# RNN input products of eight steps by seven block products, in a fused RNN and LSTM kernel on one Trainium2 core

## The reference

```python
# layer 0 (RNN), h0 = cond_1024
xW = einsum('ntd,dh->nth', x, WxR) + bR
h_t = tanh(h_{t-1} @ WhR + xW_t)
y = x + h
# layer 1 (LSTM), starts at zero
a = y_t @ WxL + bL + h_{t-1} @ WhL           # 2048 columns: i, f, o, g
c = sigmoid(f) * c + sigmoid(i) * tanh(g)
h = sigmoid(o) * tanh(c)
out = y + h
```

## Time and profile before

| | |
|---|---|
| median of 3 runs | 846.36 us (844.5 to 847.37) |
| profiled execution | 844.77 us, span of its core 843.0 us |
| TensorE busy | 827.6 us (98%), 22859 matmuls |
| TensorE's stationary loads | 620.9 us (74%) |
| VectorE / ScalarE / GpSimd busy | 602.5 / 578.9 / 289.0 us |
| granted TensorE clock | full (2.4 GHz) over the whole span |

### The profile page before, as it was taken

The page is one execution under the profiler, slowest core; times in us unless marked ns, Lnnn a source line. Parts: engine busy times, 40 slices in busy tenths (PEclk is TensorE's granted clock), DMA queues, the critical chain, the costliest instruction groups (busy, mean ns, idle before and its releaser), DMA issues.

```text
span 843.0 us, 52000 instructions
## 1 busy us (share of the span) xinstructions
PE 827.6 (98%) x22859; PEld 620.9 (74%) x22859; DVE 602.5 (71%) x1722; ACT 578.9 (69%) x1542; POOL 289.0 (34%) x642
## 2 busy tenths in 40 slices
PE   8899999999999999999999999999999999999997
PEld 5555555677787777877778777787777877778896
DVE  3668778877777776777677777668776776767664
ACT  5986476767676667767767776677767767677652
POOL 1312366723323323333332332333333233333320
PEclk9999999999999999999999999999999999999999
DMA  8801100111001111001111000111110000000001
GB/s 309 281 18 27 29 15 16 28 28 26 19 18 30 29 30 29 16 16 30 29 29 29 23 24 17 29 29 30 29 26 20 17 16 17 16 16 16 11 11 28
DMA packets 40195, 30.70 MB, mean 36 GB/s; under 512 B 5772, under 2 KB 38688, under 8 KB 38688
## 3 DMA queue, kind: packets, MB, share of 16 engines
q1 hardware_dynamic: 39712, 27.27, 11.3%
q10 hardware_dynamic: 256, 0.11, 0.0%
HBM read 18.95 MB, written 8.39 MB: 32 GB/s over the span
## 4 chain that ended last, share of the span: by engine, by line
PE 90%; DMA 4%; DVE 3%; ACT 2%; issue 1%; SPq 0%; ACTq 0%; DVEq 0%
PE ps_l L1290 34%; PE ps_l L1356 29%; PE ps_r L1442 9%; PE ps_r L1462 8%; PE ps_l L1334 3%; PE ps_l L1303 2%; PE ps_l L1323 2%; DMA wxl_raw<-in_L_cond_Wx 2%; DMA whl_raw<-in_L_cond_Wh 2%; DMA whr_raw<-in_L_cond_Wh 1%; PE ps_r L1413 1%; PE ps_r L1424 1%; DVE ig L1092 0%; PE ps_l L1277 0%; DVE fc L1090 0%
## 5 line engine op out<-in xcount | busy, mean ns | idle before, releaser
L496 POOL TENSOR_TENSOR xb<-xb,h_l 128x128 f32<-128x128 f32 x127 | 58.2, 458 | 383.8 <-DVE h_lo L1125 379.4
L1090 DVE TENSOR_TENSOR fc<-gates,c 128x128 f32<-128x128 f32 x128 | 39.6, 309 | 150.4 <-ACT gates L780 136.5
L1356 PE MATMUL ps_l<-whl_raw,wxl_raw 128*32 128x256 f16 x3816 | 131.6, 273 | 0.0
L1290 PE MATMUL ps_l<-whl_hi,hT_hi 128*32 128x512 f16 x1888 | 122.5, 379 | 1.1 <-DVE hT_hi L1109 1.1
L1290 PE MATMUL ps_l<-whl_hi,hT_lo 128*32 128x512 f16 x1888 | 122.5, 379 | 0.0
L1290 PE MATMUL ps_l<-whl_lo,hT_hi 128*32 128x512 f16 x1888 | 122.4, 379 | 0.0
L1356 PE MATMUL ps_l<-wxl_hi,wxl_raw 128*32 128x256 f16 x2544 | 115.8, 273 | 0.0
L1356 PEld LDWEIGHTS ps_l<-whl_raw,wxl_raw 128*32 128x32 f16 x3816 | 102.1, 97 | 2.2 <-issue 0.2
L780 ACT ACTIVATE gates<-ps_l,g_products 128x256 f32<-128x256 f32 x114 | 53.5, 469 | 54.2 <-PE ps_l L1290 54.1
L1290 PEld LDWEIGHTS ps_l<-whl_lo,hT_hi 128*32 128x32 f16 x1888 | 51.1, 97 | 50.8
L1290 PEld LDWEIGHTS ps_l<-whl_hi,hT_lo 128*32 128x32 f16 x1888 | 51.1, 97 | 50.8
(11 more groups left out here) (215 smaller groups left out, 1820.6 us busy)
## 6 DMA issues: line engine op xcount, KB each, us to landing
xb<-in_x SPq DMA_DIRECT2D x128, 64.0 KB, 2.2
out<-xb SPq DMA_DIRECT2D x124, 64.0 KB, 1.8
whl_raw<-in_L_cond_Wh SPq DMA_DIRECT2D x4, 1024.0 KB, 6.6
wxl_raw<-in_L_cond_Wx SPq DMA_DIRECT2D x4, 1024.0 KB, 6.0
wxr_raw<-in_L_cond_Wx SPq DMA_DIRECT2D x1, 1024.0 KB, 5.4
whr_raw<-in_L_cond_Wh SPq DMA_DIRECT2D x1, 1024.0 KB, 7.4
out<-xb SPq DMA_DIRECT2D x4, 48.0 KB, 2.2
wxl_raw<-peaks SPq DMA_DIRECT2D x5, 2.0 KB, 2.6
```

Source lines behind the costliest of these rows:

```text
L496: nc.gpsimd.tensor_tensor(xb[g % NX][:, t, :], xb[g % NX][:, t, :], h_l[s % 2][:, :], ALU.add).then_inc(out_done, 1)
L1290: last = nc.tensor.matmul(ps_l[s % 4][quarter(j), :], (hT_hi, hT_lo)[h_part][:, k, :], gate_slice(whl[w_part][k], j), start=False, stop=(h ...
L1356: last = nc.tensor.matmul(at[quarter(j), :], stationary, weights[:, j, :, :], start=False, stop=(y_part == 1 and k == 1), skip_group_check ...
```

## The change

From RNN step 48 on (XQ = 6, blocks q = 6 to 15 of eight steps) the input products are made for eight steps at once. The two groups of four steps are the two rows of a 2 x 2 block matrix, the two halves of the contraction its columns; WxR is cut into 2 x 2 blocks too. Instead of eight block products (8 * 24 matmuls) seven are made (7 * 24), one in each of the ticks 8q - 9 to 8q - 3, in the place of `product_r16`; in tick 8q - 2 there is none. They are accumulated in two PSUM banks (`ps_pk`, `ps_end`). Around them are added, for each q:

- GpSimd: four sums of 128x256 (`x_sum`, ticks 8q - 11 and 8q - 9).
- ScalarE, behind `rnn_h_hi` at the end of a tick: in 8q - 10 two high halves of 128x512 and a seed, in 8q - 9 a copy, a seed and a high half of 128x256, in 8q - 8 a copy and a high half of 128x512, in 8q - 7 a copy, in 8q - 4 and 8q - 3 a whole bank of 128x512 out of PSUM (`take_x`).
- VectorE, behind everything else of a tick: the two turns of x in 8q - 14 and 8q - 12 (before: ahead of the RNN's turn, in ticks 4g - 4), the low halves in 8q - 10 and 8q - 8, two additions in PSUM in 8q - 6 and 8q - 4.
- SyncE: twice eight transfers inside SBUF that bring the results to the partitions where the RNN's recurrent product wants them (`x_inputs`), beside zeros. `seed_xin` puts them into the RNN's PSUM bank in the place of the bias.

`x16_hi`, `x16_lo` and `product_r16` end before step 48. The blocks of WxR are made once, in ticks 27 to 33. The batches of x scales now hold two groups each from group 12 on, and come eight ticks earlier. From tick 27 on the RNN state's low half is made ahead of the LSTM's cell (fc, ig, c), not behind it. Two scale constants go from 2^-14 to 2^-12.

```diff
+XQ = 6
+GX = 2 * XQ
-        BATCHES = [(G1, 3)] + [(g, 4) for g in range(4, NG, 4)]
+        BATCHES = [(G1, 3), (4, 4), (8, 4)] + [(g, 2) for g in range(GX, NG, 2)]
-        TURN_X_AT.update({4 * g - 4: g for g in range(3, NG)})
+        TURN_X_AT.update({4 * g - 4: g for g in range(3, GX)})
-        X16_AT.update({4 * g - 2: g for g in range(RG + 1, NG)})
+        X16_AT.update({4 * g - 2: g for g in range(RG + 1, GX)})
+        LOW_FIRST = 27
+        X_ORDER = (1, 5, 6, 2, 7, 3, 4)
+        def ahead(k, ticks):
+            q = (k + ticks) // 8
+            return q if (k + ticks) % 8 == 0 and XQ <= q < NG // 2 else None
...
+            def x_inputs(q, half):                                   # SyncE
+                sp.wait_ge(x_out, 2 * (q - XQ) + half + 1)
...
+                for t in range(TG):
+                    for c in (0, 1):
+                        sp.dma_start(xin[quarter(c), 4 * half + t, :, :], ...)
...
+                if ahead(k, 11) is not None:                         # GpSimd
+                    x_sum(ahead(k, 11), 1)
+                    x_sum(ahead(k, 11), 2)
+                if ahead(k, 9) is not None:
+                    x_sum(ahead(k, 9), 3)
+                    x_sum(ahead(k, 9), 4)
...
-                if RS <= k + 2 < T:                                  # ScalarE
+                if RS <= k + 2 < 8 * XQ:
                     seed_r(k + 2)
+                if 8 * XQ <= k + 2 < T:
+                    seed_xin(k + 2)
                 if R0 - 1 <= k < T - 1:
                     rnn_h_hi(k)
+                for i in XW_HALVES_AT.get(k, []):
+                    wxr_high(i)
+                if ahead(k, 10) is not None:
+                    x_top_high(ahead(k, 10))
+                    x_sums_high(ahead(k, 10), 0)
+                    seed_xa(ahead(k, 10))
+                if ahead(k, 9) is not None:
+                    copy_xm1(ahead(k, 9))
+                    seed_xd(ahead(k, 9))
+                    x_22_high(ahead(k, 9))
+                if ahead(k, 8) is not None:
+                    take_xm5(ahead(k, 8))
+                    x_sums_high(ahead(k, 8), 1)
+                if ahead(k, 7) is not None:
+                    copy_xu2(ahead(k, 7))
+                if ahead(k, 4) is not None:
+                    take_x(ahead(k, 4), 0)
+                if ahead(k, 3) is not None:
+                    take_x(ahead(k, 3), 1)
...
+                    if LOW_FIRST <= k < T:                           # VectorE
+                        rnn_h_lo(k - 1)
                     cell(k - LAG)
...
-                    if R0 <= k < T:
+                    if R0 <= k < LOW_FIRST:
                         rnn_h_lo(k - 1)
                     hidden(k - LAG)
...
+                if ahead(k, 14) is not None:
+                    turn_block(2 * ahead(k, 14))
+                if ahead(k, 12) is not None:
+                    turn_block(2 * ahead(k, 12) + 1)
...
+                if ahead(k, 10) is not None:
+                    x_top_low(ahead(k, 10))
+                    x_sums_low(ahead(k, 10), 0)
+                if ahead(k, 8) is not None:
+                    x_22_low(ahead(k, 8))
+                    x_sums_low(ahead(k, 8), 1)
...
-                elif r < T:                                          # TensorE, next_product_r
+                elif r < 8 * XQ:
                     product_r16(r)
+                for i, n in enumerate(X_ORDER):
+                    if ahead(r - 1, 9 - i) is not None:
+                        x_block(ahead(r - 1, 9 - i), n)
```

More of the change, by code:

```diff
@@ L163, in rnn_lstm_kernel @@
         ps_end = bank("ps_end")
+        ps_x = [ps_pk, ps_end]
         s_h0 = sem("h0_loaded")
@@ new lines, in x_top_high @@
+            def x_top_high(q):
+                act.wait_ge(xg_turned, 2 * (q - XQ) + 2)
+                group_scales(act, 2 * q)
+                if q == XQ:
+                    input_product_done(act, S2 - 1)
+                    act.wait_ge(y_split, G2 - G1)
+                else:
+                    x_products_done(act, q - 1, 2)
+                nc.scalar.activation(xs_top[0], x_row(2 * q), ACT.Copy,
+                                     scale=g_scale_r[:, OF_X, 2 * q:2 * q + 1]).then_inc(xs_high, 1)
@@ L757, in rnn_h_hi, with take_x @@
+            def take_x(q, half):
+                x_products_done(act, q, 4 if half else 3)
+                wait(act, xin_loaded[half], DMA * 2 * TG * (q - XQ))
+                nc.scalar.activation(x_wide[half], ps_x[half][:, :], ACT.Copy).then_inc(x_out, 1)
             def rnn_h_hi(r):
@@ L1209, in _ @@
                     add_u3(pair_at(k - 1))
+                if ahead(k, 14) is not None:
+                    turn_block(2 * ahead(k, 14))
+                if ahead(k, 12) is not None:
+                    turn_block(2 * ahead(k, 12) + 1)
+                for i in XW_HALVES_AT.get(k, []):
+                    wxr_low(i)
+                if ahead(k, 10) is not None:
[4 more added lines that the diff above has]
+                    x_sums_low(ahead(k, 8), 1)
+                if ahead(k, 6) is not None:
+                    add_xm5(ahead(k, 6))
+                if ahead(k, 4) is not None:
+                    add_xu3(ahead(k, 4))
                 if k == T:
@@ L1430, in quadrant_of_r16, with x_block @@
                 return w[:, chunk * H:(chunk + 1) * H].rearrange("p (m c u) -> p c m u", m=2, c=2)[:, c, :, :]
+            def x_block(q, n):
+                done = 4 * (q - XQ)
+                if n == 1:
+                    pe.wait_ge(xs_split, done + 1)
+                    pe.wait_ge(xa_seeded, q - XQ + 1)
+                elif n == 5:
+                    if q == XQ:
+                        pe.wait_ge(xw_split, J)
+                    pe.wait_ge(xs_split, done + 2)
+                    pe.wait_ge(xd_seeded, q - XQ + 1)
+                elif n == 6:
+                    pe.wait_ge(xm1_copied, q - XQ + 1)
+                elif n in (2, 7):
+                    pe.wait_ge(xs_split, done + 4)
+                    pe.wait_ge(xm5_out, q - XQ + 1)
+                    pe.wait_ge(xu2_copied, q - XQ + 1)
+                elif n == 3:
+                    pe.wait_ge(xb_sum, q - XQ + 1)
+                else:
+                    pe.wait_ge(xd_sum, q - XQ + 1)
+                out = {1: (0, 0), 2: (0, 0), 6: (0, 1), 3: (0, 1), 5: (1, 1), 7: (1, 0), 4: (1, 0)}[n]
+                cols = slice(out[1] * HALF, (out[1] + 1) * HALF)
+                x_home, x_at = {1: (xs_top, 0), 2: (xs_top, HALF), 4: (xs_22, 0), 5: (xs_sums, 0), 6: (xs_sums, HALF),
+                                7: (xs_sums, 2 * HALF), 3: (xs_sums, 3 * HALF)}[n]
+                w_home, w_row, w_at = {1: (wr[OF_X], 0, 0), 2: (wr[OF_X], 2, HALF), 3: (wr[OF_X], 2, 0), 5: (tx, 0, 0),
+                                       7: (tx, 0, HALF), 6: (tx, 2, 0), 4: (tx, 2, HALF)}[n]
+                for x_part, w_part in ((0, 0), (0, 1), (1, 0)):
+                    for k in (0, 1):
+                        first = (w_row + k) * H + w_at
+                        for t in range(TG):
+                            at = x_at + k * P + t * B
+                            last = nc.tensor.matmul(ps_x[out[0]][quarter(t), cols], x_home[x_part][:, at:at + B],
+                                                    w_home[w_part][:, first:first + HALF], start=False,
+                                                    stop=(x_part == 1 and k == 1), skip_group_check=True)
+                last.then_inc(xp_mm, 1)
             def recurrent_r16(r):
```

214 lines of the change are left out of this document (202 added, 12 removed).

## The result

The changed kernel takes 855.88 us (median of 6 runs, 855.49 to 859.84), the kernel before 845.95 (6 runs, 844.5 to 847.37): ratio 1.0125, 95% interval 1.0104 to 1.0146. It is slower by 1.25%. The profiled execution took 855.49 us, its span is 853.7, 10.7 more than the 843.0 of before. The lines of the page, changed kernel: span, busy times, shares of the chain that ended last, and the transfers of `x_inputs` (KB each, us to landing).

A forecast was written before the change was run, and what follows sets the result against it. TensorE was taken as the bound, with 0.81 us of slack a tick behind it. -6.35 + 10.9 + 1.7 + 1.0 = +7.3 us gave 852.0 for the profiled execution, 853.6 on the median, said as 854; range 842 to 863.

The forecast's parts named there:

- What bounds: Kernel before: TensorE alone sets the pace, 6.19 us a tick; the ScalarE and VectorE chain has 0.81 us slack.
- TensorE's account, -6.35: Steps 48 to 127: 240 matmuls fewer, 6.56 us, against about 0.21 for one bank fill.
- The filling of one PSUM bank: 512 columns over the whole array on TensorE, said to cost about 0.21 us.
- Stalls in the block: TensorE waits for hT_hi from tick 8q - 2 on, 1.34 us a block against 0.66 saved; 10.9 us over all blocks.
- The third: Stall in tick 8q' - 9, behind a copy, a seed and a high half: 0.1 us.
- The first and last blocks, and q = 6: Stalls of 0.7 us in the first block, 0.8 in the last; the blocks of q = 6 cost nothing.
- GpSimd, 1.7: x_sum beside VectorE slows fc by 0.19 us once a period, nine times: 1.7 us, bounds 0 and 5.
- Once, 1.0: High and low halves of WxR's blocks, ticks 32 and 33: fc late in 33, 1.0 us, 0 to 2.
- SyncE, nothing: x_inputs: eight transfers take 3.6 us to issue and 2.6 to landing, of some 10.8 us; nobody waits.
- Low half early: RNN's low half ahead of the cell: costs nothing in a usual tick, wins nothing.
- A: Rival: TensorE stays the bound, added work disappears in idle time, 6.35 us come out: 840.0; chance 0.14.

The follow-up runs named there:

- spread: Changed kernel with second take_x, sums' high halves and seeds moved between xr and h_r, other halves to neighbouring ticks: 841.16 us, 0.9960 of the kernel before.
- filler_back: Changed kernel with 24 matmuls of 256 columns put back into tick 8q - 2 of blocks 7 to 14: 855.62 us, 1.0115 of the kernel before.
- no_sums: Changed kernel with GpSimd's x_sum made for q = 6 alone, old sums reused: 853.94 us, 1.0098 of the kernel before.
- spread_setup: `spread` with WxR blocks made one a tick (27 to 34), their high halves between xr and h_r: 839.21 us, 0.9933 of the kernel before.
- no_transfers: Changed kernel without the x_inputs transfers from q = 7 on, seeds reading old inputs: 856.20 us, 1.0136 of the kernel before.
- before_low_first: Kernel before with only the RNN state's low half made ahead of the LSTM's cell from tick 27 on: 844.88 us, ratio 1.0000.
- low_last: Changed kernel with the RNN state's low half made behind the cell again in all ticks: 860.77 us, 1.0172 of the kernel before.

## Why the prediction was right

854 was said, 855.9 came, by the mechanism that was named. The change itself was put at +7.3 us and measured at +9.9. The forecast came closer than that because it started from 846.4 where the median is now 845.95, and was rounded up by 0.4. The range of 842 to 863 holds the time of the kernel before too, so what bears the prediction out is the direction and the account of the ticks. By its steps:

- **What bounds.** Shown: with the added instructions out of the way (`spread`) TensorE's 0.66 us a block come out in full; where they stand, TensorE's work is free (`filler_back`).
- **TensorE's account, -6.35.** Right within 0.25: eight ticks of `spread` are 0.66 shorter. Ticks 118 to 125 of the changed kernel take 5.53 to 5.54 each, as said; tick 126, counted with them, takes 6.19 against 6.84 before, also 0.65 less. The filling of one PSUM bank cost twice what was said: ticks 29 and 30 take 0.43 more than before, not 0.21, and between them stands, in the instructions in order of time,

```profile
198.48 0.39 PE L1829 MATMUL ps_pk<-ident 128*128 128x512 f16 x1
```

  The load behind it, at 198.79, names no other engine as its releaser, and hT_hi had been ready since 197.62.
- **Stalls in the block.** Predicted 0.40, 0.62, 0.10, 0.22, none; measured 0.53, 0.58, 0.41, 0.19, 0.10. Four of five are within 0.13. (The 0.10 of the third was rounded up: its own times, 16.10 and 16.06, give 0.04.) The third was mis-sized: the loss of 0.19 to GpSimd was put once a period somewhere, and it falls on L1213 in this tick at 0.27, which `no_sums` gives back. With that term the block was 1.53 predicted and is 1.81 measured. Eight ticks take 50.68, just above the 50.2 to 50.4 said.
- **The first and last blocks, and q = 6.** By starts of the loads of hT_hi (after less before), ticks 46 to 118 lose 9.5 us where TensorE's account alone gives back 8 * 0.66 = 5.25: 14.7 of stalls. Said were 10.9 + 1.7 = 12.6. The first block has 1.1 of it (0.7 said), the last 1.1 (0.8 said), the seven between 1.8 each. The blocks of q = 6 cost nothing beside their products, as said: from tick 39 to 47 the changed kernel loses 4.58 us, which is seven products of 0.655. The gates of tick 46 are 0.5 us late behind `take_x`, but that tick is not shortened and TensorE doesn't wait.
- **GpSimd, 1.7.** `no_sums` shows 0.28 a block, 2.5 in nine: within the bounds. The reading behind it was too mild: the mean of fc, 482 ns, mixes short and long overlaps, and the loss for each is what is left of GpSimd's instruction, as above.
- **Once, 1.0.** The most mis-sized of the terms: 1.7 us in ticks 33 to 35. The instructions in order of time, ticks 32 and 33, changed kernel:

```profile
214.80 0.54 DVE L1370 TENSOR_TENSOR fc<-gates,c 128x128 f32<-128x128 f32 x1
...
220.08 1.13 ACT L919 ACTIVATE wxl_raw<-whl_raw 128x512 f16<-128x512 f32 x2
...
220.72 1.29 DVE L1166 TENSOR_TENSOR wxl_raw<-whl_raw,wxl_raw 128x512 f16<-128x512 f32 x2 [0.99 <-ACT wxl_raw L919]
...
221.12 0.45 ACT L996 ACTIVATE gates<-ps_l,g_products 128x256 f32<-128x256 f32 x1
...
222.20 0.28 DVE L1370 TENSOR_TENSOR fc<-gates,c 128x128 f32<-128x128 f32 x1
```

  I priced one tick, that with a peak. But the two low halves at the end of tick 32 end at 222.01, and fc behind them starts 7.40 us after the last one; the next two do the same in tick 33. Each of the two ticks stalls, by 0.7 and 1.1. `spread_setup` gives 1.2 of it back.
- **SyncE, nothing.** Right in cost (`no_transfers`), wrong in the issue time: 5.5 to 7.5 us, not 3.6. The room was larger than said as well, 11.8 us in the block shown (from the end of `take_x` at 553.64 to the seed at 565.40), so that the margin was 3 to 4 us as a rule and 1.6 in the tightest block, where 4.6 was said.
- **Low half early.** "Costs nothing in a usual tick" is shown by `before_low_first`; that it wins in late ticks (some 5 us, `low_last`) I had not counted.

In sum, from the trace: TensorE's account -6.1 (-6.35 said), stalls 14.7 (12.6), once 1.7 (1.0), and 0.4 at the start and the end, which vary from one execution to the next: 10.7 us. All terms were low by a little. Of the rivals A is what happens when most of the same instructions stand elsewhere, not here.
The Trainium skill (Perfetto Trace Analysis, section "Identifying the Most-Contended Engine") has the most occupied engine as the one to relieve first, and judges TensorE by its stationary loads instead of its matmuls. By that too TensorE came first, though only with 74% against VectorE's 71%. A relief of 6.35 us for it lost 10 us, and it paid only once most of the work added in exchange stood elsewhere.

## What to carry to other kernels

Where two recurrent chains run behind a busy engine, price added work by the slack of the chain at the place where it is queued (here 0.81 us a tick), not by the idle share of its engine. Look inside the tick for the gap in which that engine waits for another one of the same chain, and queue new instructions there. Here the added work cost 1.81 us a block with all of it at the end of ticks, and nothing once the long instructions had moved into gaps and to neighbouring ticks. A tick that is emptied of the bound engine's work brings its gain only if nothing is queued ahead of its chain just then.

## What the runs showed of the hardware

- Eight transfers of 32 KB inside SBUF take SyncE 5.5 to 7.5 us to issue in the changed kernel, 0.7 to 0.9 each, where the earlier trace rows has 1.78 us for four stores. Without them nothing got faster (`no_transfers`).
- A VectorE instruction with two inputs in SBUF that starts during a GpSimd instruction takes longer by what that one has left, less 0.18 or 0.19 us: L1213 by 0.27 with 0.45 left, L1218 of `spread_setup` by 0.79 with 0.98 left. For fc it is the same with 0.14: 0.54 instead of 0.28 at 214.80, with 0.40 left. It goes the other way too: GpSimd's sum that starts during L1213 takes 1.00 instead of 0.73.
- ScalarE at 128x512 with a scale operand takes 0.71, without one 0.58; in the rows of ticks 85 and 86 the next instruction starts 0.06 to 0.11 before the end of the last.
- One matmul of 512 columns over the whole array between matmuls of 32-column tiles cost 0.43 us, where its own record is 0.39 and a quarter of the array takes 0.054 for 512 columns at the same clock (48 in 2.59 us).
